# Moving GpSimd's two long additions, the softmax sums and half of the output projection inside one attention step

## The chip, the cores and the metric

The kernel runs on one core of one Trainium2 chip. The metric is device time in microseconds from the first to the last instruction and what lies around them. Each engine (TensorE, VectorE, ScalarE, GpSimd, SyncE for DMA issues) has its own instruction stream, written out by hand, and semaphores tie the streams together.

## The reference

64 independent blocks b, each of 256 rows by 256 columns, pass through cross attention over 120 context rows of 192 columns, and then through a quantised feed-forward layer (FFN):

```python
x = x + xattn(layernorm(x), ctx)       # 8 heads of 32: softmax(q k^T / sqrt(32)) v, then @ Wo + bo
x = x + ffn(layernorm(x))              # ln * g1 + b1n, int8-like rows, ternary w1 (1024), gelu,
                                       # ln * g2 + b2n, quantised rows, ternary w2, + b2
```

Quantising a row means dividing it by its largest absolute value over 127 and rounding.

## The kernel before

The program has two long stages. The attention stage takes steps i = -5 to 63, and every step works on several blocks at once, each at another point of its way. The FFN stage follows and is not touched by the change; between them stands a written-out piece for the last blocks. Steps 24 to 58 or so are in a hardware loop that holds four steps; the others are written out. In steps 4 to 21 some set-up work for the FFN weights is hung behind the steps ("aside").

One step of the attention stage, i, by engine, in the order of the code:

- TensorE (`attn` at the end of the file): raw scores of block i (L1237, `raw_ps` is signalled at their end), values of i-1 (L1264), projection of i-2 with Wo into `y_p` (L1317, `y_ps`), turning the partial maxima of i (L1244), softmax sums of i-1 (L1273, `sum_ps`), the shift that subtracts the maxima from the scores in PSUM (L1250, waits for `nmt_done`, signals `sc_ps`), keys and values of i+2 (`keys_values`: V's first product L1283, then K's from L1286, which wait for `x1_done`), queries of i+2 (L1307, `kvq_ps`), and the spreading of the inverse sums of i-1 (L1298).
- VectorE: the affine part of the FFN's layer norm of i-3 in two halves (L697, `h`), the maxima of the raw scores (L686, `nm_part`, waits for `raw_ps`), `h_max`, `nm_row`, `nm_t` (L724, which multiplies the maxima by the constant `block_sel`), the addition of `y_p` to the residual rows `xr` of i-2 (L730, waits for `y_ps`, signals `x1_done`), the inverse of the sums (L739), statistics, centring of `h` (L762), then `q_t` of i+2 (L774, waits for `kvq_ps`) and `o_t` of i-1 (L783).
- GpSimd: the inverse deviations of x of block i+3 (three small instructions L506, L508, L511, `r_done`), two additions over 512 columns, b2 to `xr` of i-3 (L489) and bo to `xr` of i-1 (L484), the quantisation of `h` of i-3 (L495, L497, waits for `h_scaled`), the power for `f_r` of i-2 (L525).
- ScalarE: copies, squares of x, the exponentials (L983, wait for `sc_ps`), `inv_hi`, the rounded rows.
- SyncE issues the DMAs in the order of its code: the turned rows, `ctx_t`, `xt`, `x_in`, then the store of `x_r` (waits for `r_done`), the load of `xr`, the store of `xr`, and the load of `r_bc`.

The PSUM bank of `y_p` is shared with `k_p`: K's products of i+2 may not start before VectorE has added `y_p` of i-2.

Of the kernel before, what the change touches and what calls it, by code (L numbers as in the profile page):

```python
# [49 lines left out]
def xattn_ffn(nc, KV, x, x_t, ctx_t_in, wq, wk, wv, wo, bo, ln1_g, ln1_b, w1, b1, ln2_g, ln2_b, w2, b2, out):  # L50
# [15 lines left out]
    with ExitStack() as ctx:  # L66
        def sb(name, shape, dt=F32, scope=ctx):
            return scope.enter_context(nc.sbuf_tensor(name, shape, dt))
# [20 lines left out]
        block_sel = sb("block_sel", [P, RB])  # L89
# [245 lines left out]
        with nc.Block() as block:  # L335
# [96 lines left out]
            def _(pool):  # L432
# [68 lines left out]
                def attn(i, n):  # L501
                    p, q = n % 2, 1 - n % 2
                    b = i + 3
# [8 lines left out]
                    b = i - 3  # L512
                    if live(b, NB):
                        add_b2(b, (n + 1) % 4)
                    b = i - 1
                    if live(b, NB):
                        add_bo(b, (n + 3) % 4)
# [84 lines left out]
            def _(dve):  # L602
# [16 lines left out]
                dve.tensor_reduce(block_sel[:, :], head_map[:, :, :, :].rearrange("p c j b -> p b c j"), AX.XY, ALU.add).then_inc(s_head, 1)  # L619
                dve.wait_ge(s_head, 3)  # L620
                dve.tensor_copy(head_sel[:, :, :], head_row[:, :].unsqueeze(2).to_broadcast([P, C, KP])).then_inc(s_head, 1)

# [507 lines left out]
            def _(pe):  # L1130
# [148 lines left out]
                def keys_values(b, p):  # L1279
# [3 lines left out]
                    pe.matmul(v_p, ctx_t[:, p, 0, 0:KV], w_kv[:, 1, :], start=True, stop=False)  # L1283
                    after(pe, x1_done, b - 3)
# [25 lines left out]

                def project(b, p):
                    pe.wait_ge(q_done, left(b + 4))
                    pe.wait_ge(k_done, left(b + 4))
                    pe.wait_ge(on_done, b + 1)
                    for t in range(T):
                        for c in range(C):
                            last = pe.matmul(y_p[:, t, :], o_t[:, p, c, t * P:(t + 1) * P],  # L1317
                                             wo_sb[:, c, :], start=(c == 0), stop=(c == C - 1))
                    last.then_inc(y_ps, 1)

                def attn(i, n):
# [5 lines left out]
                    if live(i - 1, NB):  # L1327
                        values(i - 1, (n + 3) % 4)
                    if live(i - 2, NB):
                        project(i - 2, p)  # L1330
                    if live(i, NB):
                        turn_minima(i)
                    if live(i - 1, NB):
                        sums(i - 1, q)
                    if live(i, NB):
                        shift(i)
                    if live(i + 2, NB):
                        keys_values(i + 2, p)
                        queries(i + 2, p)
# [79 lines left out]
```

## Time and profile before

| | us |
|---|---|
| median of 3 runs (lowest, highest) | 1227.91 (1223.06, 1230.76) |
| the profiled execution | 1227.72 |
| its span | 1226.0 |
| busy: VectorE, TensorE, ScalarE, GpSimd | 1128.3, 999.6, 815.4, 715.9 |

The granted clock of TensorE is 0.968 of full speed over the span. The attention stage is the part up to about 720 us, the FFN stage the rest. In the timelines below each line is the start in us from the span's start, the duration, the engine, the line of the code, the operation, the output and the inputs, the shapes, the count of merged instructions, and in brackets the idle time before it with what ended it.

### The profile page before, as it was taken

How to read it: one execution, taken by the hardware profiler on the slowest of the kernel's cores; microseconds unless marked ns; L12 is line 12 of the kernel's file. 1: busy time of each engine (PE TensorE's matmuls, PEld its weight loads, DVE VectorE, ACT ScalarE, POOL GpSimd, SP SyncE). 2: the span in 40 equal slices, each digit the busy share in tenths (PEclk: the TensorE clock that was granted, in tenths of full speed). 3: DMA queues.
4: the chain of work that ended last, by engine and by line, in shares of the span. 5: the costliest groups of instructions: out<-in, count | busy, mean ns of one | idle time of the engine just before them, and what ended most of it. 6: DMA issues, size and time to landing. Idle time of an engine off the chain costs nothing.

```text
span 1226.0 us, 29427 instructions
## 1 busy us (share of the span) xinstructions
PE 999.6 (82%) x9649; PEld 667.1 (54%) x9649; DVE 1128.3 (92%) x1718; ACT 815.4 (67%) x2083; POOL 715.9 (58%) x924
## 2 busy tenths in 40 slices
PE   5888888888888988888898876788777777777776
PEld 4566656656666666666666643444444444444444
DVE  2789998989999999999998989999999999999997
ACT  3555544555555555555554447799999999999993
POOL 3355644554555555555554544677777677767775
PEclk8999999989999999999999978899999999999998
DMA  5567765556666655666665430133222332233224
GB/s 141 137 149 149 164 133 107 133 111 132 141 141 135 130 127 134 137 136 140 135 136 115 100 91 18 26 36 42 35 34 34 40 37 34 34 39 38 34 35 69
DMA packets 144472, 114.63 MB, mean 93 GB/s; under 512 B 51580, under 2 KB 134908, under 8 KB 144408
## 3 DMA queue, kind: packets, MB, share of 16 engines
q1 hardware_dynamic: 126824, 96.90, 35.7%
q0 software_dynamic: 16864, 16.26, 11.2%
q8 instruction: 36, 0.59, 0.3%
q10 hardware_dynamic: 720, 0.66, 0.2%
q14 instruction: 28, 0.23, 0.1%
HBM read 71.75 MB, written 33.63 MB: 86 GB/s over the span
## 4 chain that ended last, share of the span: by engine, by line
DVE 43%; PE 30%; issue 24%; DVEq 1%; ACT 1%; POOL 1%; DMA 1%; POOLq 0%; ACTq 0%
DVE nm_part L686 11%; PE banks L1307 10%; DVE h L697 7%; DVE gn_low L810 6%; DVE gn_high L810 6%; PE banks L1273 5%; PE banks L1283 3%; DVE o_t L783 3%; PE banks L1286 2%; PE banks L1250 2%; DVE gn_low L796 2%; DVE gn_high L796 2%; PE banks L1288 2%; DVE q_t L774 1%; DVE g_max L816 1%
## 5 line engine op out<-in xcount | busy, mean ns | idle before, releaser
L983 ACT ACTIVATE probs<-banks 120x512 f32<-120x512 f32 x256 | 137.6, 590 | 168.7 <-PE banks L1250 168.7
L686 DVE TRANSPOSE_TENSOR_REDUCE nm_part<-banks 128x64 f16<-128x2048 f32 x64 | 147.4, 2302 | 3.5 <-PE banks L1237 3.2
L1021 ACT ACTIVATE g_dev<-g,g_sum 128x1024 bf16<-128x1024 f32 x128 | 149.1, 1165 | 0.0
L1026 ACT ACTIVATE g<-banks,h_dq 128x1024 f32<-128x1024 f32 x128 | 142.4, 1129 | 8.8 <-PE banks L1184 8.8
L1202 PE MATMUL banks<-w_t,g_t 128*128 128x256 bf16 x1008 | 125.2, 279 | 14.6 <-ACT g_t L1059 12.1
L495 POOL COPY h_dq<-h_cl 128x2 f32<-128x2 f32 (+1 forms) x64 | 13.7, 214 | 207.0 <-DVE h_qs L734 204.0
L1178 PE MATMUL banks<-w_t,h_t 128*128 128x512 bf16 x512 | 127.8, 394 | 2.0 <-ACT g L1026 1.3
L1307 PE MATMUL banks<-xt,wq_c 128*128 128x256 f32 x512 | 128.5, 394 | 0.0
L1317 PE MATMUL banks<-wo_sb,o_t 128*128 128x256 f32 x512 | 127.6, 392 | 1.0 <-DVE o_t L844 1.0
L1202 PEld LDWEIGHTS banks<-w_t,g_t 128*128 128x128 f16 x1008 | 95.7, 100 | 54.4 <-issue 26.9
L525 POOL TENSOR_TENSOR f_r<-f_ve,neg_half 128x2 f32<-128x2 f32 x62 | 50.0, 806 | 108.7 <-DVE f_ve L766 108.7
L1317 PEld LDWEIGHTS banks<-wo_sb,o_t 128*128 128x128 f32 x512 | 92.0, 189 | 37.3 <-issue 27.4
L558 POOL TENSOR_TENSOR g_r<-g_ve,neg_half 128x2 f32<-128x2 f32 x64 | 104.5, 1633 | 10.2 <-ACT g_ve L1042 10.2
L697 DVE SCALAR_TENSOR_TENSOR h<-h,f_r,b1n_bc 128x256 f32<-128x256 f32 x122 | 107.8, 923 | 0.1
L1307 PEld LDWEIGHTS banks<-xt,wq_c 128*128 128x128 f32 x512 | 92.7, 191 | 18.3 <-issue 0.9
L989 ACT ACTIVATE k_t<-banks 128x256 f32<-128x256 f32 x64 | 24.5, 383 | 114.1 <-DVE q_t L774 114.1
L484 POOL TENSOR_TENSOR xr<-xr,bo_bc 128x512 f32<-128x512 f32 x64 | 89.5, 1399 | 5.6 <-DMA xr<-in_x 5.6
L489 POOL TENSOR_TENSOR xr<-xr,b_bc 128x512 f32<-128x512 f32 x64 | 91.9, 1436 | 0.0
L533 POOL TENSOR_TENSOR g_dq<-g_max,w_out 128x2 f32<-128x2 f32 x64 | 12.5, 196 | 130.7 <-DVE gn_low L810 70.3
L774 DVE TENSOR_TENSOR q_t<-banks,r_bc 128x512 f32<-128x512 f32 x64 | 44.3, 692 | 47.7 <-PE banks L1307 38.8
L1244 PE MATMUL banks<-ident_h,nm_part 128*128 128x128 f16 x64 | 13.9, 217 | 88.0 <-DVE nm_part L686 88.0
L1196 PE MATMUL banks<-ident_h,gn_low 128*128 128x128 f16 x512 | 40.3, 224 | 51.2 <-POOL gn_low L538 51.2
(165 smaller groups left out, 2798.0 us busy)
## 6 DMA issues: line engine op xcount, KB each, us to landing
x_in<-in_x SPq DMA_DIRECT2D x64, 256.0 KB, 3.2
xt<-in_x_t SPq DMA_DIRECT2D x64, 256.0 KB, 2.9
xr<-in_x SPq DMA_DIRECT2D x64, 256.0 KB, 6.0
out<-xr SPq DMA_DIRECT2D x64, 256.0 KB, 6.2
out<-res POOLq DMA_DIRECT2D x62, 256.0 KB, 4.3
ctx_t<-in_ctx_t SPq DMA_DIRECT2D x64, 128.0 KB, 2.2
r_bc<-r_rows SPq DMA_DIRECT2D x64, 128.0 KB, 4.7
w_raw<-in_w_t SPq DMA_DIRECT2D x8, 256.0 KB, 5.4
```

The costliest lines, as they stand in the source:

```text
L489: pool.tensor_tensor(xr[:, r, :, :], xr[:, r, :, :], b2_bc[:, :].unsqueeze(1).to_broadcast([P, T, D]), ALU.add).then_inc(b2_done, 1)
L558: pool.tensor_tensor(g_r[:, q, :], g_ve[:, q, :], neg_half[:, 0:T], ALU.pow).then_inc(gr_done, 1)
L686: dve.tensor_reduce(nm_part[:, :, 0:C * RB], blocks_p, AX.X, ALU.max, negate=True, apply_transpose=True).then_inc(max_done, 1)
L697: last = dve.scalar_tensor_tensor(out=h[:, r1, t, :], in0=h[:, r1, t, :], scalar=f_r[:, q, t:t + 1], in1=b1n_bc[:, :], op0=ALU.mult, op1=A ...
L810: dve.scalar_tensor_tensor(out=gn[n][:, t, :], in0=gn[n][:, t, :], scalar=g_r[:, p, t:t + 1], in1=b2n_bc[:, :], op0=ALU.mult, op1=ALU.add) ...
L983: act.activation(probs[:, p, j, :, :], sc_p[0:KV, j, :, :], ACT.Exp, scale=SCALE).then_inc(probs_done, 1)
L1021: act.activation(g_dev[:, t, :], g[:, p, t, :], ACT.Square, scale=-float(F), bias=g_sum[:, p, t:t + 1], accum_out=g_ssq[:, p, t:t + 1]).th ...
L1026: act.activation(g[:, p, t, :], u_p[t], ACT.Gelu, scale=h_dq[:, b, t:t + 1], accum_out=g_sum[:, p, t:t + 1]).then_inc(gelu_done, 1)
L1178: pe.matmul(u_p[t][:, cols], h_t[:, b, t * C + c, :], w1_t[:, c, cols], start=(c == 0), stop=False, skip_group_check=True)
L1202: pe.matmul(y[t], turned_rows[:, t, f, :], w2_t[:, f, :], start=(first and f == 0), stop=False, skip_group_check=True)
L1307: last = pe.matmul(q_p[:, m, :], wq_c[:, c, m * P:(m + 1) * P], xt[:, p, c, :], start=(c == 0), stop=(c == C - 1))
L1317: last = pe.matmul(y_p[:, t, :], o_t[:, p, c, t * P:(t + 1) * P], wo_sb[:, c, :], start=(c == 0), stop=(c == C - 1))
```

## The change

Five edits:

1. GpSimd's additions of b2 and bo move to the head of its step, ahead of the three small instructions of x, and wait for `raw_ps` of this step.
2. TensorE's softmax sums of i-1 move up, directly behind the values of i-1.
3. The projection of i-2 is split by tile of 128 rows: tile 0 ahead of the turned maxima, tile 1 behind them. `y_ps` is signalled at the end of tile 1.
4. V's first product of i+2 moves ahead of the shift.
5. `block_sel` becomes 16-bit: `block_row` holds the 32-bit sums, and one more copy is made at the start.

```diff
@@ block_sel
-        block_sel = sb("block_sel", [P, RB])
+        block_row = sb("block_row", [P, RB])
+        block_sel = sb("block_sel", [P, RB], F16)
@@ gpsimd
                 def attn(i, n):
                     p, q = n % 2, 1 - n % 2
+                    if live(i, NB) and live(i - 1, NB):
+                        pool.wait_ge(raw_ps, i + 1)
+                    b = i - 3
+                    if live(b, NB):
+                        add_b2(b, (n + 1) % 4)
+                    b = i - 1
+                    if live(b, NB):
+                        add_bo(b, (n + 3) % 4)
                     b = i + 3
                     if live(b, NB):
                         pool.wait_ge(x_ssq, b * T + T)
...
                         pool.tensor_tensor(x_r[:, q, :], x_ve[:, q, :], neg_half[:, 0:T], ALU.pow).then_inc(r_done, 1)
-                    b = i - 3
-                    if live(b, NB):
-                        add_b2(b, (n + 1) % 4)
-                    b = i - 1
-                    if live(b, NB):
-                        add_bo(b, (n + 3) % 4)
@@ vector, at the start
-                dve.tensor_reduce(block_sel[:, :], head_map[:, :, :, :].rearrange("p c j b -> p b c j"), AX.XY, ALU.add).then_inc(s_head, 1)
+                dve.tensor_reduce(block_row[:, :], head_map[:, :, :, :].rearrange("p c j b -> p b c j"), AX.XY, ALU.add).then_inc(s_head, 1)
...
+                dve.tensor_copy(block_sel[:, :], block_row[:, :]).then_inc(s_head, 1)
+                dve.wait_ge(s_head, 5)
@@ tensor
-                def keys_values(b, p):
+                def first_values(b, p):
                     after(pe, q_done, b)
                     after(pe, v_done, b)
                     pe.wait_ge(ctx_loaded[p], (b - p) * 8 + 16)
                     pe.matmul(v_p, ctx_t[:, p, 0, 0:KV], w_kv[:, 1, :], start=True, stop=False)
+
+                def keys(b, p):
                     after(pe, x1_done, b - 3)
...
+                def project_tile(b, t, p):
+                    if t == 0:
+                        pe.wait_ge(q_done, left(b + 4))
+                        pe.wait_ge(k_done, left(b + 4))
+                        pe.wait_ge(on_done, b + 1)
+                    for c in range(C):
+                        last = pe.matmul(y_p[:, t, :], o_t[:, p, c, t * P:(t + 1) * P],
+                                         wo_sb[:, c, :], start=(c == 0), stop=(c == C - 1))
+                    if t == T - 1:
+                        last.then_inc(y_ps, 1)
...
                         values(i - 1, (n + 3) % 4)
+                        sums(i - 1, q)
                     if live(i - 2, NB):
-                        project(i - 2, p)
+                        project_tile(i - 2, 0, p)
                     if live(i, NB):
                         turn_minima(i)
-                    if live(i - 1, NB):
-                        sums(i - 1, q)
+                    if live(i - 2, NB):
+                        project_tile(i - 2, 1, p)
+                    if live(i + 2, NB):
+                        first_values(i + 2, p)
                     if live(i, NB):
                         shift(i)
                     if live(i + 2, NB):
-                        keys_values(i + 2, p)
+                        keys(i + 2, p)
                         queries(i + 2, p)
```

TensorE in one step of the loop, from the values to K's first products, before (in brackets the semaphores that an instruction waits for):

```order
L1264 MATMUL banks<-probs,v_sb 32x256 x7
L1317 MATMUL banks<-wo_sb,o_t 128x256 [waits on_done,k_done,q_done]
L1317 MATMUL banks<-wo_sb,o_t 128x256 x3
L1244 MATMUL banks<-ident_h,nm_part 128x128 [waits max_done,o_done]
L1273 MATMUL banks<-probs,sum_sel 32x128 [waits on_done]
L1273 MATMUL banks<-probs,sum_sel 32x128 x15
L1250 MATMUL banks<-nm_t,head_sel 128x256 [waits nmt_done]
L1250 MATMUL banks<-nm_t,head_sel 128x256 x7
L1283 MATMUL banks<-w_kv,ctx_t 120x256 [waits ctx_loaded0,v_done,q_done]
L1286 MATMUL banks<-ctx_t,w_kv 128x128 [waits x1_done]
```

The same stretch of the changed program, whose line numbers are a few higher:

```order
L1269 MATMUL banks<-probs,v_sb 32x256 x7
L1278 MATMUL banks<-probs,sum_sel 32x128 [waits on_done]
L1278 MATMUL banks<-probs,sum_sel 32x128 x15
L1324 MATMUL banks<-wo_sb,o_t 128x256 [waits on_done,k_done,q_done]
L1324 MATMUL banks<-wo_sb,o_t 128x256
L1249 MATMUL banks<-ident_h,nm_part 128x128 [waits max_done,o_done]
L1324 MATMUL banks<-wo_sb,o_t 128x256 x2
L1288 MATMUL banks<-w_kv,ctx_t 120x256 [waits ctx_loaded0,v_done,q_done]
L1255 MATMUL banks<-nm_t,head_sel 128x256 [waits nmt_done]
L1255 MATMUL banks<-nm_t,head_sel 128x256 x7
L1293 MATMUL banks<-ctx_t,w_kv 128x128 [waits x1_done]
```

Between the turned maxima and K's products there stood the 16 sum products, the shift and V's product; now two projection products, V's product and the shift stand there.

GpSimd in one step of the loop, before:

```order
L506 TENSOR_TENSOR x_var<-x_dev,inv_d 128x2 [waits x_ssq]
L508 TENSOR_TENSOR x_ve<-x_var,eps_t 128x2 [waits r_chain]
L511 TENSOR_TENSOR x_r<-x_ve,neg_half 128x2 [waits r_stored1,r_chain]
L489 TENSOR_TENSOR xr<-xr,b_bc 128x512 [waits h_centred]
L484 TENSOR_TENSOR xr<-xr,bo_bc 128x512 [waits xr_loaded1]
```

And in the changed program:

```order
L490 TENSOR_TENSOR xr<-xr,b_bc 128x512 [waits h_centred,raw_ps]
L485 TENSOR_TENSOR xr<-xr,bo_bc 128x512 [waits xr_loaded1]
L515 TENSOR_TENSOR x_var<-x_dev,inv_d 128x2 [waits x_ssq]
L517 TENSOR_TENSOR x_ve<-x_var,eps_t 128x2 [waits r_chain]
L520 TENSOR_TENSOR x_r<-x_ve,neg_half 128x2 [waits r_stored1,r_chain]
```

The two long additions are ahead of the three small instructions, and the first of them has the new wait.

## Rows read from the trace of the kernel before

**Rows 1.** The chain of waits, 363 to 378 us: start, us, what.

```profile
365.72 1.01 PE banks L1273 x32
...
368.81 1.94 PE banks L1307 x8
...
372.37 1.49 DVE h L697
```

**Rows 2.** Timeline of VectorE over one step of the loop, 363 to 378 us.

```profile
363.06 2.30 DVE L686 TRANSPOSE_TENSOR_REDUCE nm_part<-banks 128x64 f16<-128x2048 f32 x1
...
366.23 0.42 DVE L724 TENSOR_TENSOR nm_t<-nm_row,block_sel 128x256 f16<-128x256 f16 x1
366.57 0.68 DVE L730 TENSOR_TENSOR xr<-banks,xr 128x512 f32<-128x512 f32 x1
...
370.77 0.69 DVE L774 TENSOR_TENSOR q_t<-banks,r_bc 128x512 f32<-128x512 f32 x1 [0.29 <-PE banks L1307]
...
373.79 2.30 DVE L686 TRANSPOSE_TENSOR_REDUCE nm_part<-banks 128x64 f16<-128x2048 f32 x1
```

**Rows 3.** Timeline of TensorE's matmuls, same stretch.

```profile
365.65 1.08 PE L1273 MATMUL banks<-probs,sum_sel 120*32 120x128 f32 x32
366.71 0.40 PE L1250 MATMUL banks<-nm_t,head_sel 32*128 32x256 f16 x8
367.04 0.69 PE L1283 MATMUL banks<-w_kv,ctx_t 128*120 128x256 f32 x2
367.57 0.61 PE L1286 MATMUL banks<-ctx_t,w_kv 128*128 128x128 f32 x4
...
368.74 1.99 PE L1307 MATMUL banks<-xt,wq_c 128*128 128x256 f32 x8
370.57 0.39 PE L1298 MATMUL banks<-inv_part,spread 128*128 128x128 f16 x4
370.89 1.15 PE L1237 MATMUL banks<-q_t,k_t 32*128 32x256 f32 x16
...
376.24 0.22 PE L1244 MATMUL banks<-ident_h,nm_part 128*128 128x128 f16 x1 [1.28 <-DVE nm_part L686]
```

**Rows 4.** Timeline of VectorE, 371.95 to 372.2 and 372.5 to 373 us: the two halves of L697.

```profile
371.98 0.47 DVE L697 SCALAR_TENSOR_TENSOR h<-h,f_r,b1n_bc 128x256 f32<-128x256 f32 x1
...
372.37 1.49 DVE L697 SCALAR_TENSOR_TENSOR h<-h,f_r,b1n_bc 128x256 f32<-128x256 f32 x1
```

**Rows 5.** Timeline of GpSimd, same step.

```profile
367.49 0.18 POOL L495 COPY h_dq<-h_cl 128x2 f32 x1 [3.23 <-DVE h_qs L734]
...
371.63 0.69 POOL L511 TENSOR_TENSOR x_r<-x_ve,neg_half 128x2 f32<-128x2 f32 x1 [0.16 <-POOL x_ve L508]
372.29 1.30 POOL L489 TENSOR_TENSOR xr<-xr,b_bc 128x512 f32<-128x512 f32 x1
373.55 1.44 POOL L484 TENSOR_TENSOR xr<-xr,bo_bc 128x512 f32<-128x512 f32 x1
```

**Rows 6.** DMA issues: operation, count, size, us to landing.

```profile
xr<-in_x SPq DMA_DIRECT2D x64, 256.0 KB, 6.0
...
r_rows<-x_r SPq DMA_DIRECT2D x64, 1.0 KB, 4.6
```

**Rows 7.** Timelines of VectorE and GpSimd in an early step, 51.9 to 57 us.

```profile
51.92 0.69 DVE L774 TENSOR_TENSOR q_t<-banks,r_bc 128x512 f32<-128x512 f32 x1 [0.55 <-PE banks L1307]
...
53.13 2.94 DVE L697 SCALAR_TENSOR_TENSOR h<-h,f_r,b1n_bc 128x256 f32<-128x256 f32 x2
56.00 2.30 DVE L686 TRANSPOSE_TENSOR_REDUCE nm_part<-banks 128x64 f16<-128x2048 f32 x1
...
53.10 1.27 POOL L489 TENSOR_TENSOR xr<-xr,b_bc 128x512 f32<-128x512 f32 x1
```

**Rows 8.** Timelines of VectorE and GpSimd, 161 to 167 and 188 to 192.6 us.

```profile
162.11 0.69 DVE L774 TENSOR_TENSOR q_t<-banks,r_bc 128x512 f32<-128x512 f32 x1 [0.39 <-PE banks L1307]
...
166.34 2.30 DVE L686 TRANSPOSE_TENSOR_REDUCE nm_part<-banks 128x64 f16<-128x2048 f32 x1
...
188.54 0.69 DVE L774 TENSOR_TENSOR q_t<-banks,r_bc 128x512 f32<-128x512 f32 x1 [1.87 <-PE banks L1307]
...
191.66 2.31 DVE L686 TRANSPOSE_TENSOR_REDUCE nm_part<-banks 128x64 f16<-128x2048 f32 x1
...
188.39 1.27 POOL L489 TENSOR_TENSOR xr<-xr,b_bc 128x512 f32<-128x512 f32 x1
```

More of the change, by code:

```diff
@@ L1309, in queries @@
                     last.then_inc(kvq_ps, 1)
+                def project_tile(b, t, p):
[8 more added lines that the diff above has]
+                        last.then_inc(y_ps, 1)
                 def project(b, p):
-                    pe.wait_ge(q_done, left(b + 4))
-                    pe.wait_ge(k_done, left(b + 4))
-                    pe.wait_ge(on_done, b + 1)
                     for t in range(T):
[L1316 to L1319, printed above, removed]
+                        project_tile(b, t, p)
                 def attn(i, n):
```

## The prediction

> **What bounds the kernel now.** The busy shares name VectorE, but a share is an average, so I read the chain of waits first, in the middle of the hardware loop [rows 1]. There the chain changes hands twice a step: TensorE holds it from the turned maxima through the sums and the shift to the queries, VectorE from `q_t` over the second half of `h` (L697) to the maxima. The timelines of the same step give the lengths. One step is 373.79 - 363.06 = 10.73 us [rows 2]. Call T the end of the maxima, 363.06 + 2.30 = 365.36, and Q the start of `q_t`, 370.77. The half-step T to Q lasts 5.41 us and TensorE sets it: VectorE stands idle for 0.29 us ahead of `q_t` and the queries end that wait [rows 2]. The half-step Q to the next maxima lasts 3.02 us and VectorE sets it, and the maxima themselves take 2.30; TensorE waits 1.28 us there [rows 3]. So TensorE work that lies in the second half is free up to 1.28 us, TensorE work in the first half is not, and VectorE's first half has 0.29 us to spare.
>
> The two halves of `h` must be read one by one [rows 4]: the first takes 0.47 us, the second 1.49. GpSimd's addition of b2 runs from 372.29 to 373.59 [rows 5]; the second half starts at 372.37 and ends at 373.86, so it did nothing until the addition was over. That is 1.49 - 0.47 = 1.02 us of every step lost to a collision. The first half, started before the addition, lost nothing.
>
> **Edit 1, the additions.** Do they leave the collision? The new wait is for the scores, which run from 370.89 to 372.04 [rows 3], that is to Q + 1.27. An engine follows a signal 0.06 us later (end of `nm_t` at 366.65, shift at 366.71) to 0.15 us later (maxima at 365.36, first sum at 365.65 with the turned maxima between); I take 0.1, so the addition of b2 starts at about Q + 1.4. It starts now at Q + 1.52 [rows 2, 5]. The halves of `h` start at Q + 1.21 and Q + 1.60 [rows 4]. The wait thus puts the addition 0.1 us earlier, still behind the first half's start and ahead of the second's: the 1.02 us stays. The addition of bo stays under the maxima. Gain: nothing.
>
> What stands behind the new wait: the three small instructions of x now follow 2.7 us of additions. `r_done` moves from Q + 1.55 to about Q + 5.5. SyncE's queue has the store of `x_r`, then the load and the store of `xr`, then `r_bc` behind that signal, so all move by some 4 us. The load of `xr` needs 6.0 us to land [rows 6]: issued at about Q + 6.2, there at Q + 12.2, wanted by the addition of bo at Q + 10.7 + 2.7 = Q + 13.4. `r_bc` is issued once the store of `x_r` has landed, 4.6 us later, and its reader `q_t` is one and a half steps away. GpSimd itself idles 3.23 us ahead of the quantisation [rows 5], which covers the 1.3 us of small instructions. All of it is hidden; cost nothing. If the cover of `xr` (1.2 us) goes, the additions slip under `h_max` and cost nothing either until GpSimd's idle time is used up.
>
> **Edits 2 and 3, sums and projection.** The sums (1.01 us of the chain, [rows 1]) leave the first half, and tile 1 of the projection comes in. The queries are eight products of the same shape: 370.57 - 368.74 = 1.83 us, some 0.22 each and 0.1 more for the first, whose weights are loaded in the open [rows 3]. Tile 1 is four such products: 0.97 us. On TensorE alone this is a draw. In the second half the sums replace tile 1, also a draw, under the 1.28 us.
>
> But `y_ps` now comes at the end of tile 1. Tile 1 starts where the sums did, T + 0.29. Eight products need 370.77 - 368.74 = 2.03 us from their first start to VectorE's start behind them; four need 2.03 - 4 x 0.22 = 1.15. VectorE's addition L730 can start at T + 1.44 instead of T + 1.21 (366.57 - 365.36): late by 0.23. It takes 0.68, so `x1_done` comes at T + 2.12, and K's first product follows 0.06 later, at T + 2.18. It starts at T + 2.21 today [rows 3]. Its weights are then loaded in the open, 0.1 us as above. K, the other products and the queries keep their 3.20 us (370.77 - 367.57). So Q comes at about T + 2.28 + 3.20 = T + 5.5 instead of 5.41: **0.1 us longer a step.** TensorE's own road would be shorter (edit 4), but it waits for VectorE. VectorE, late by 0.23, uses up 0.23 of its idle 0.29 and stays ahead of the queries, which are late too.
>
> **Edit 4, V's product.** It takes 0.53 us (367.57 - 367.04) and moves from behind the shift to before it [rows 3]. The sums' last products and the shift leave a hole of about 0.1 us now, since the shift follows `nm_t`; with tile 1 and V ahead, the shift starts at T + 0.29 + 0.97 + 0.43 = T + 1.7, well behind `nm_t` at T + 1.29. TensorE would be at K by T + 2.0, which is 0.2 us earlier than today, and waits there for `x1_done`. The gain lands on that wait. The exponentials start 0.35 us later; ScalarE has over 1 us idle a step, so nothing.
>
> **Edit 5, 16 bits.** `nm_t` takes 0.42 us for 256 columns with one 32-bit input [rows 2]. Shorter or not, VectorE then waits at L730 for `y_ps`, so it counts zero. 
>
> **The early steps.** In six steps before 280 us TensorE was slow or late, and the addition of b2 began before the scores were done and was over before `h`. One is the step at 188: b2 from 188.39 to 189.66, and 191.66 - 188.54 = 3.12 us from `q_t` to the maxima. A step with the same work in which b2 met `h` took 166.34 - 162.11 = 4.23 [rows 8]. The new wait makes the first kind into the second: at most 1.1 us each, at least nothing. I take 0.7 x 6 = 4 us (bounds 0 and 6.6).
>
> **Sum.** Of 64 steps some 57 have all the parts: 57 x 0.1 = 6 us. With 4 us in the early steps: +10 us on the profiled 1227.72, which is the median of the runs (1227.91) within 0.2. Forecast 1237 us. The step's term has bounds of -0.05 (weights loaded under the wait: Q at T + 5.38) and +0.2 (VectorE starts later behind `y_ps`), so -3 to +11 us, and with the early steps 1225 to 1246.
>
> **Rival A: the collision goes** (faster). Should the addition of b2 begin behind the second half of `h`, VectorE has 1.02 us less a step, and TensorE's slack of 1.28 covers it: 57 x 1.02 = 58 us, 1170. For it: the maxima and the addition now wait for the same signal. Against it: the signal comes 0.33 us ahead of the second half. Chance 0.07.
>
> **Rival B: both halves collide** (slower). If `q_t` falls 0.15 us or more behind the scores, the addition starts ahead of the first half, bo takes the second, and nothing is left under the maxima. The step at 52 us shows it [rows 7]: b2 at 53.10, `h` at 53.13, both halves 2.94 us, 56.00 - 51.92 = 4.08 us from `q_t` to the maxima instead of 3.02. Price 1.06 x 57 = 60 us, 1298; in the ten or so written-out full steps alone, 1248. It decides at 0.1 to 0.2 us of lateness of VectorE against the queries; I have it 0.1 ahead. The Trainium skill, "SBUF — State Buffer", section on who interferes with whom, says that a VectorE instruction with two SBUF inputs and a reading GpSimd instruction exclude each other for a whole instruction, and that issue order decides; rows 4 and 7 agree with it (0.47 and 1.49 us in one order, 2.94 in the other). Chance 0.11 for all of it or the written-out part.
>
> **Rival C: the wait for `y_ps` is shorter than I have it** (faster). Should L730 not be late, the 0.2 us of edit 4 come through: 57 x 0.19 = 11 us less, with the early steps 1221. It needs tile 1 to take 0.25 us less than the queries' products of the same shape. Chance 0.17.
>
> **Clock.** The mean granted clock is 0.968; a stretch at the lower level (1.2 instead of 2.4 GHz) costs a few us, and a change in TensorE's gaps can add or drop one. That is 5 us either way inside each case.
>
> **How the numbers follow.** Forecast (1225 to 1246) 0.55, C 0.17, B 0.11, A 0.07, things I did not see 0.10. A range from 1214 to 1258 holds the forecast, C, the small form of B and half of the unseen, 0.8. This kernel's measurement tells about 1% from no change, 12 us: 1215.6 to 1240.2. Forecast 0.36 within and 0.19 above; C 0.11 within, 0.06 below; A 0.07 below; B 0.10 above; the unseen in thirds. Faster 0.20, same 0.48, slower 0.32.
>
> **What would show it.** In the profile after: a step of 10.8 us in the loop; the second half of `h` still at 1.5 us with b2 starting at Q + 1.4; L730 with some 0.2 us idle ahead of it that tile 1 ends; K's first product behind L730; six early steps longer. A second half of `h` at 0.47 us proves A, a first half over 1 us proves B, a step under 10.6 with no wait at L730 proves C.

## The result and the profile after

| | before | changed |
|---|---|---|
| median, us (lowest, highest, runs) | 1225.5 (1223.06, 1230.76, 4) | 1241.26 (1239.48, 1247.94, 4) |
| ratio [95% interval] | | 1.0133 [1.0084, 1.0183] |
| the profiled execution, its span | 1227.72, 1226.0 | 1247.94, 1246.3 |
| granted clock over the span | 0.968 | 0.960 |

The kernel is 1.3% slower, 16 us by the medians. The profiled execution of the changed kernel is its slowest, and its granted clock, 0.960, is the lowest measured for this kernel (0.963 to 0.968 in its other executions). So the 20.3 us between the two spans are 4.5 more than the medians give, and what is said below of the clock's share holds for this execution. I read the two traces against each other, stage by stage first.

A step is named here by the block whose `q_t` begins it. The stretches run from one `q_t` to another: blocks 5 to 24 (written out), 24 to 58 (the loop, and two steps ahead of it) and 58 to 63. Columns are length, busy us of TensorE's matmuls, its weight loads, VectorE, ScalarE and GpSimd, then the granted clock, the DMA share and GB/s. Before:

```profile
65.35:284.48 219.13, 187.70 (x2001) 134.24 (x1999) 199.34 (x395) 115.10 (x327) 114.65 (x170) 0.96 0.64 136
284.48:649.94 365.46, 321.45 (x3572) 229.61 (x3570) 346.19 (x681) 200.35 (x579) 192.16 (x307) 1.00 0.62 134
649.94:706.21 56.27, 48.72 (x527) 34.66 (x525) 51.62 (x104) 25.82 (x69) 30.28 (x53) 0.97 0.49 107
```

The same stretches of the changed kernel:

```profile
61.19:294.03 232.84, 193.47 (x2001) 136.17 (x1999) 207.75 (x396) 114.10 (x327) 121.45 (x174) 0.93 0.59 129
294.03:663.22 369.19, 321.21 (x3572) 229.05 (x3570) 350.71 (x681) 198.05 (x579) 197.25 (x306) 1.00 0.59 133
663.22:724.75 61.53, 52.94 (x527) 37.23 (x525) 52.85 (x105) 25.55 (x69) 31.39 (x53) 0.89 0.50 101
```

The loss is not in the loop, where most of the steps are (+3.7 us over 34 steps), but in the written-out steps on both sides of it (+13.7 and +5.3), and there the granted clock is lower. Ahead of block 5 the changed kernel gains 4.2 us: 2.6 of them in the step at 52 us, where both halves of `h` had collided [rows 7] and which now has b2 behind the first half, and 1.6 before it. Behind block 63 another 1.8 us are added, which is no more than the kernels below differ by there (517.4 to 521.5 us).

**The loop step.** The chain of waits, start, us and what, answering [rows 1], changes hands at the same places:

```profile
381.05 1.94 PE banks L1314 x8
...
384.61 1.50 DVE h L702
```

VectorE in one step of the loop, answering [rows 2]; then TensorE, answering [rows 3]:

```profile
375.26 2.30 DVE L691 TRANSPOSE_TENSOR_REDUCE nm_part<-banks 128x64 f16<-128x2048 f32 x1
...
378.43 0.42 DVE L729 TENSOR_TENSOR nm_t<-nm_row,block_sel 128x256 f16<-128x256 f16 x1
...
378.95 0.69 DVE L735 TENSOR_TENSOR xr<-banks,xr 128x512 f32<-128x512 f32 x1
...
383.01 0.69 DVE L779 TENSOR_TENSOR q_t<-banks,r_bc 128x512 f32<-128x512 f32 x1
...
386.04 2.30 DVE L691 TRANSPOSE_TENSOR_REDUCE nm_part<-banks 128x64 f16<-128x2048 f32 x1
```

```profile
377.71 0.22 PE L1249 MATMUL banks<-ident_h,nm_part 128*128 128x128 f16 x1 [1.28 <-DVE nm_part L691]
377.76 1.08 PE L1324 MATMUL banks<-wo_sb,o_t 128*128 128x256 f32 x4
...
379.21 0.40 PE L1255 MATMUL banks<-nm_t,head_sel 32*128 32x256 f16 x8
...
379.70 0.71 PE L1293 MATMUL banks<-ctx_t,w_kv 128*128 128x128 f32 x4
```

T is 375.26 + 2.30 = 377.56 and Q is 383.01. The addition L735 (L730 before) starts at T + 1.39 instead of T + 1.21; it ends at 379.64 and K's first product follows at 379.70. The step is 10.78 us long (10.77 on average), 0.04 over the one before. TensorE's wait ahead of the turned maxima is 1.28 us, as before.

The halves of `h`, answering [rows 4], and GpSimd, answering [rows 5]:

```profile
384.22 0.47 DVE L702 SCALAR_TENSOR_TENSOR h<-h,f_r,b1n_bc 128x256 f32<-128x256 f32 x1
...
384.61 1.50 DVE L702 SCALAR_TENSOR_TENSOR h<-h,f_r,b1n_bc 128x256 f32<-128x256 f32 x1
```

```profile
384.38 1.45 POOL L490 TENSOR_TENSOR xr<-xr,b_bc 128x512 f32<-128x512 f32 x1 [0.96 <-PE banks L1242]
...
387.84 0.71 POOL L520 TENSOR_TENSOR x_r<-x_ve,neg_half 128x2 f32<-128x2 f32 x1 [0.16 <-POOL x_ve L517]
```

The addition of b2 now waits for the scores and starts at Q + 1.37, and the second half of `h` still stands behind it for 1.50 us.

**An early step.** VectorE, GpSimd and TensorE between 171 and 184 us, to be held against [rows 8]:

```profile
171.68 0.69 DVE L779 TENSOR_TENSOR q_t<-banks,r_bc 128x512 f32<-128x512 f32 x1 [0.28 <-PE banks L1314]
...
175.85 2.30 DVE L691 TRANSPOSE_TENSOR_REDUCE nm_part<-banks 128x64 f16<-128x2048 f32 x1
...
180.49 0.69 DVE L735 TENSOR_TENSOR xr<-banks,xr 128x512 f32<-128x512 f32 x1 [1.04 <-PE banks L1324]
...
174.19 1.45 POOL L485 TENSOR_TENSOR xr<-xr,bo_bc 128x512 f32<-128x512 f32 x1
...
178.30 0.27 PE L1249 MATMUL banks<-ident_h,nm_part 128*128 128x128 f16 x1 [2.53 <-DVE nm_part L691]
178.37 2.02 PE L1324 MATMUL banks<-wo_sb,o_t 128*128 128x256 f32 x4
```

In these steps set-up work stands ahead of `h`, so it is addition bo, not b2, that takes the second half. The maxima start 4.17 us behind `q_t`, as in the step at 162 before (4.23). TensorE then waits 2.53 us, and behind that wait its products take twice their time (four of L1324: 2.02 us instead of 1.08): it has been granted 1.2 GHz instead of 2.4. So L735 waits 1.04 us more, and the step takes 13.4 us.

### The profile page after: what moved, and what is told of

Same layout as the page of the kernel before. It is cut to its first block, busy times and chain, and to the rows that moved or that the text cites. A ratio compares the mean times of both kernels' runs of the same rounds, so it can differ in the third digit from the quotient of the medians.

```text
span 1246.3 us, 29490 instructions
## 1 busy us (share of the span) xinstructions
PE 1007.4 (81%) x9649; PEld 671.1 (54%) x9649; DVE 1139.0 (91%) x1719; ACT 812.8 (65%) x2083; POOL 715.0 (57%) x924
## 4 chain that ended last, share of the span: by engine, by line
DVE 47%; PE 25%; issue 23%; POOL 3%; DVEq 1%; DMA 1%; ACT 0%; POOLq 0%; ACTq 0%
DVE nm_part L691 11%; PE banks L1314 10%; DVE h L702 8%; DVE gn_low L815 6%; DVE gn_high L815 6%; PE banks L1324 4%; PE banks L1293 4%; DVE o_t L788 3%; DVE xr L735 3%; DVE gn_high L801 2%; PE banks L1295 2%; POOL gn_high L541 1%; DVE gn_low L801 1%; DVE q_t L779 1%; PE banks L1297 1%
## 5 line engine op out<-in xcount | busy, mean ns | idle before, releaser
L1324 PE MATMUL banks<-wo_sb,o_t 128*128 128x256 f32 x512 | 149.6, 418 | 0.9 <-DVE o_t L849 0.9
L490 POOL TENSOR_TENSOR xr<-xr,b_bc 128x512 f32<-128x512 f32 x64 | 98.4, 1537 | 63.6 <-PE banks L1242 63.6
L702 DVE SCALAR_TENSOR_TENSOR h<-h,f_r,b1n_bc 128x256 f32<-128x256 f32 x122 | 115.8, 990 | 0.1
L1324 PEld LDWEIGHTS banks<-wo_sb,o_t 128*128 128x128 f32 x512 | 91.2, 198 | 22.0 <-issue 14.0
L561 POOL TENSOR_TENSOR g_r<-g_ve,neg_half 128x2 f32<-128x2 f32 x64 | 91.4, 1428 | 10.3 <-ACT g_ve L1047 10.3
L801 DVE SCALAR_TENSOR_TENSOR gn_low<-g,g_nm,g_bc 128x1024 f32<-128x1024 f32 x64 | 81.3, 1277 | 0.0
```

Source lines behind the costliest of these rows:

```text
L490: pool.tensor_tensor(xr[:, r, :, :], xr[:, r, :, :], b2_bc[:, :].unsqueeze(1).to_broadcast([P, T, D]), ALU.add).then_inc(b2_done, 1)
L702: last = dve.scalar_tensor_tensor(out=h[:, r1, t, :], in0=h[:, r1, t, :], scalar=f_r[:, q, t:t + 1], in1=b1n_bc[:, :], op0=ALU.mult, op1=A ...
L801: dve.scalar_tensor_tensor(out=gn[n][:, t, :], in0=g[:, p, t, :], scalar=g_nm[:, p, t:t + 1], in1=g2_bc[:, :], op0=ALU.add, op1=ALU.mult). ...
```

## Where the 20 us are

Two things can be summed over the steps of the two traces: the time from `q_t` to the maxima, which a collision lengthens, and the time at the lower clock. The price of the latter comes from experiment 5 below: 0.39 us for each us. A collision is one of the two long additions of GpSimd holding up a half of `h`.

| stretch | longer, us | `q_t` to maxima, sum | time at 1.2 GHz | worked out |
|---|---|---|---|---|
| blocks 5 to 14 | 0.5 | | none in either | 9 steps of 0.05 |
| 14 to 24 | 13.3 | 36.5 to 43.2 | 17.1 to 34.1 | 6.8 + 17.0 x 0.39 = 13.4 |
| 24 to 58 | 3.7 | +1.1 in one step | 0 to 3.4 | 1.1 + 1.3 + 33 x 0.04 = 3.7 |
| 58 to 63 | 5.3 | +1.5 in one step | 3.4 to 13.6 | 1.5 + 4.0 = 5.5 |

The two prices hold beyond the pair of kernels that gave them. From block 14 to 24 the length of the stretch runs from 107.9 to 135.6 us over the fourteen profiles of this document; less the sum from `q_t` to the maxima and less 0.39 us for each us at 1.2 GHz it is 78.7 to 79.9 us in every one.

The one loop step is that of block 29, whose `q_t` is at 348.00 us. The loop's first pass ends there:

```profile
349.41 3.02 DVE L702 SCALAR_TENSOR_TENSOR h<-h,f_r,b1n_bc 128x256 f32<-128x256 f32 x2
...
349.46 1.28 POOL L490 TENSOR_TENSOR xr<-xr,b_bc 128x512 f32<-128x512 f32 x1 [1.04 <-PE banks L1242]
...
354.81 0.22 PE L1249 MATMUL banks<-ident_h,nm_part 128*128 128x128 f16 x1 [2.61 <-DVE nm_part L691]
```

Both halves collide there, as in rival B, and the step takes 13.46 us. `q_t` is not late against the scores: they end at Q + 1.26, as in every loop step. It is `h` that comes late, at Q + 1.41 instead of 1.20, and it does so in the kernel before as well. So the addition, at Q + 1.45, began 0.044 us behind the first half's start by the records, and still went ahead of it.

## Experiments

All are compared with the kernel before on their own chip; its medians were 1225.54, 1224.21 and 1227.64 us in the three groups of runs. Times of stretches come from each kernel's profiled execution.

**1. Edit 1 alone.** The kernel before with GpSimd's new order and wait, nothing else:

```diff
+                    if live(i, NB) and live(i - 1, NB):
+                        pool.wait_ge(raw_ps, i + 1)
+                    b = i - 3
+                    if live(b, NB):
+                        add_b2(b, (n + 1) % 4)
...
```

> The kernel before with edit 1 alone (the two additions at the head of GpSimd's step, behind the scores). Theory: edit 1 costs nothing in the loop (step 10.73 us, second half of h 1.49 us as before) and carries most of the loss through the steps before 280 us, where the additions now meet h: 1234 to 1240 us, and the maxima start about 4.2 us behind q_t in the steps with weight work, not 3.1 to 3.6. Rival: the loss comes from TensorE's new order (edits 2 to 4), and this kernel takes 1224 to 1229 us.

Measured: 1238.03 us, as expected, ratio 1.0109 [1.0082, 1.0136]. Loop steps take 10.73 us, as before; blocks 5 to 24 take 231.4 us instead of 219.1, blocks 58 to 63 59.5 instead of 56.3. VectorE, then GpSimd, in a loop step:

```profile
379.08 0.69 DVE L776 TENSOR_TENSOR q_t<-banks,r_bc 128x512 f32<-128x512 f32 x1 [0.29 <-PE banks L1309]
...
382.10 2.30 DVE L688 TRANSPOSE_TENSOR_REDUCE nm_part<-banks 128x64 f16<-128x2048 f32 x1
...
380.45 1.44 POOL L489 TENSOR_TENSOR xr<-xr,b_bc 128x512 f32<-128x512 f32 x1 [1.12 <-PE banks L1239]
```

The addition starts at Q + 1.37 and the maxima at Q + 3.02: nothing is won in the loop, and the written-out steps lose.

This trace prices the clock without any added work. The step of block 17 has the same collision and the same wait of TensorE (2.53 us) as that of block 15, but no time at 1.2 GHz: it takes 11.98 us against 13.56 with 3.4 us at that level, 0.46 us lost for each us. So the lower level does not follow every such wait either.

**2. The other edits alone.** The changed kernel with edit 1 undone (the hunk of experiment 1 reversed, so that the three small instructions stand ahead of the additions again).

> The changed kernel with edit 1 undone (GpSimd as before; sums, projection, V's product and the 16-bit constant as changed). Theory: the loop's step is 10.77 us instead of 10.73 from the wait for tile 1 ahead of L730, which makes 2 to 3 us in all: 1227 to 1231 us, early steps as before. Rival: TensorE's order carries the loss, 1236 to 1242 us, with the lower clock as often as in the changed kernel.

Measured: 1210.51 us, 0.9881 [0.986, 0.9903]. My expectation failed: this half of the change is a gain of 1.2%, which edit 1 takes away. Blocks 5 to 24 are longer than before (226.2 us), but the loop takes 343.7 us instead of 365.5. Two steps of it, VectorE and then GpSimd:

```profile
508.65 0.69 DVE L777 TENSOR_TENSOR q_t<-banks,r_bc 128x512 f32<-128x512 f32 x1
...
509.86 0.87 DVE L700 SCALAR_TENSOR_TENSOR h<-h,f_r,b1n_bc 128x256 f32<-128x256 f32 x2
...
518.40 0.69 DVE L777 TENSOR_TENSOR q_t<-banks,r_bc 128x512 f32<-128x512 f32 x1
...
519.61 1.94 DVE L700 SCALAR_TENSOR_TENSOR h<-h,f_r,b1n_bc 128x256 f32<-128x256 f32 x2
...
510.32 1.55 POOL L490 TENSOR_TENSOR xr<-xr,b_bc 128x512 f32<-128x512 f32 x1
...
519.98 1.28 POOL L490 TENSOR_TENSOR xr<-xr,b_bc 128x512 f32<-128x512 f32 x1
```

In the first step b2 starts at Q + 1.67 and both halves together take 0.87 us; in the second at Q + 1.58 and they take 1.94. The second half of `h` starts at Q + 1.60. GpSimd's small instructions follow work of VectorE that comes behind L730, and L730 is 0.18 us later while Q is only 0.04 later: that moves the addition from Q + 1.52 to the edge of the collision. Some 23 of the 34 steps are clear of it and take 9.75 us, the others 10.83.

**3. The addition behind `h`, in the kernel before.** One line ahead of the addition of b2:

```diff
+                        pool.wait_ge(h_affine, b + 1)
                         add_b2(b, (n + 1) % 4)
```

> The kernel before, with the addition of b2 made to wait until both halves of h of the same block are done (h_affine), nothing else changed. Theory: the collision is worth its full 1.02 us a step, since TensorE has 1.28 us to spare there: step 9.7 us, both halves 0.47 us, about 58 us less, 1165 to 1175 us. Rival: something else takes over after a part of it (the additions run into the next work of GpSimd, or TensorE's queue), and a step is 10.2 us or more, 1195 us or more.

Measured: 1163.24 us, 0.9487 [0.9461, 0.9513], a little under the expected range. VectorE, GpSimd and TensorE in the loop:

```profile
466.96 0.69 DVE L775 TENSOR_TENSOR q_t<-banks,r_bc 128x512 f32<-128x512 f32 x1 [0.29 <-PE banks L1308]
...
468.17 0.87 DVE L698 SCALAR_TENSOR_TENSOR h<-h,f_r,b1n_bc 128x256 f32<-128x256 f32 x2
...
469.12 1.27 POOL L489 TENSOR_TENSOR xr<-xr,b_bc 128x512 f32<-128x512 f32 x1 [0.59 <-DVE h L698]
...
471.41 0.22 PE L1245 MATMUL banks<-ident_h,nm_part 128*128 128x128 f16 x1 [0.26 <-DVE nm_part L687]
...
476.68 0.69 DVE L775 TENSOR_TENSOR q_t<-banks,r_bc 128x512 f32<-128x512 f32 x1 [0.29 <-PE banks L1308]
```

The step is 476.68 - 466.96 = 9.72 us. The 1.02 us of the collision are gone, TensorE's wait falls from 1.28 to 0.26 by the same amount, and the addition of b2 runs under the maxima at no cost: it takes 1.27 us beside them. Rival A's price was right; its condition is not one that the change makes.

**4. The same in the changed kernel**, in place of the wait for the scores:

```diff
-                    if live(i, NB) and live(i - 1, NB):
-                        pool.wait_ge(raw_ps, i + 1)
                     b = i - 3
                     if live(b, NB):
+                        pool.wait_ge(h_affine, b + 1)
                         add_b2(b, (n + 1) % 4)
```

> The changed kernel with its wait for the scores replaced by the same wait for both halves of h. Theory: the additions' place at the head of the step is harmless and the signal was the wrong one: both halves 0.47 us, step 9.75 us, 1168 to 1180 us, some 4 us behind the kernel before with that wait. Rival: with the small instructions of x behind the additions, r_done and the load of xr come too late once the step is 9.7 us, and GpSimd waits for the load; then 1190 us or more.

Measured: 1163.22 us, 0.9496 [0.9475, 0.9518], the same as experiment 3 and 5 us below the expected range. Loop steps take 9.75 us instead of 9.72. So edits 2 to 5 show no gain of their own once the collision is gone; what they did in experiment 2 was to move the addition. Between the two kernels stands the semaphore for which b2 waits: 1241 us with the scores, 1163 with `h`.

**5. Work in TensorE's gap.** To tell the clock from the collisions, the changed kernel computes tile 0 of the projection three times instead of once in the written-out steps 12 to 22, 60 and 61. Nothing is left out; the two copies overwrite the same values, and TensorE has less time to wait.

```diff
                         project_tile(i - 2, 0, p)
+                        if isinstance(i, int) and (12 <= i <= 22 or i in (60, 61)):
+                            project_tile(i - 2, 0, p)
+                            project_tile(i - 2, 0, p)
```

> The changed kernel with tile 0 of the projection computed twice more in steps 12 to 22, 60 and 61: the same values into the same place, 1.9 us of TensorE work ahead of the turned maxima, where it waited over 2.5 us in those steps. Theory: the lower clock follows these waits; with work in them it stays high in the early steps, and each of some nine early steps is 2.5 us shorter, minus up to 0.5 us where the added work ends too late: 15 to 25 us less than the changed kernel, 1216 to 1227 us. Rival: the collisions of the additions alone make the loss and the clock falls as often for other reasons: 1241 us or more.

Measured: 1229.69 us, 1.0025 [1.0003, 1.0046]. That is 11.6 us less than the changed kernel by the medians, where I expected 15 to 25: the direction was right and the size too large. Blocks 5 to 24:

```profile
62.54:283.58 221.04, 199.20 (x2089) 145.68 (x2087) 207.85 (x396) 113.91 (x327) 120.92 (x174) 0.99 0.65 135
```

TensorE does 88 products more, as the trace counts them, and the stretch is 11.8 us shorter than in the changed kernel, with a granted clock of 0.99 instead of 0.93. The collisions are unchanged: from block 14 to 24 the sum from `q_t` to the maxima is 43.2 and 43.3 us, while the time at 1.2 GHz is 3.4 us instead of 34.1 and the stretch 123.7 us instead of 135.6. That is 11.9 / 30.7 = 0.39 us lost for each us at the lower level. TensorE in one of these steps:

```profile
178.48 0.22 PE L1249 MATMUL banks<-ident_h,nm_part 128*128 128x128 f16 x1 [0.80 <-DVE nm_part L691]
...
178.53 1.08 PE L1324 MATMUL banks<-wo_sb,o_t 128*128 128x256 f32 x4
```

The wait is 0.80 us instead of 2.53 and tile 1 takes 1.08 instead of 2.02.

**6. Edit 1 only from step 24 on**, in the changed kernel: `late = not isinstance(i, int) or i >= 24` decides whether the additions stand at the head with the wait or behind the small instructions.

> The changed kernel, with edit 1 in force from step 24 on only (before it GpSimd keeps the old order without the wait). Theory: in the loop edit 1 pins the addition of b2 to Q + 1.37, ahead of the second half of h, so every loop step stays at 10.77 us; the early steps lose less TensorE time and less clock than in the changed kernel, 5 to 10 us: 1231 to 1237 us. Rival: the loss against the kernel with TensorE's edits alone (1210) is made in the early steps, and this kernel takes 1210 to 1218 us.

Measured: 1235.78 us, 1.009 [1.0054, 1.0125]. Blocks 5 to 24 take 228.6 us, so only 4.2 of the 13.7 come back: the other edits lengthen these steps too, as experiment 2 showed (226.2; the code of these steps is the same, so 2.4 us is what two profiles of it differ by). In experiment 1 edit 1 alone made them 231.4. Each edit is enough to move the addition out of the lucky places that it had before in four of these steps (b2 over before `h` began), and the losses don't add. In the step of block 29 both halves collided again.

**7. Additions at the head, no wait**, in the kernel before: edit 1's hunk without its first two lines.

> The kernel before with the two additions at the head of GpSimd's step and no wait for the scores. Theory: the addition of b2 begins right behind f_r, at about Q + 0.3, and ends at Q + 1.6; the first half of h (Q + 1.2) waits for its end, the addition of bo then meets the second half: the two halves take 2.0 to 2.4 us together, a step 10.8 to 11.2 us, 1228 to 1250 us. Rival: the addition of b2 is over before it hurts and bo alone collides as b2 did: step 10.73, 1223 to 1228 us.

Measured: 1214.41 us, 0.9928 [0.99, 0.9956]. I expected slower. VectorE and GpSimd in the loop:

```profile
502.91 1.98 DVE L697 SCALAR_TENSOR_TENSOR h<-h,f_r,b1n_bc 128x256 f32<-128x256 f32 x2
...
501.94 1.26 POOL L489 TENSOR_TENSOR xr<-xr,b_bc 128x512 f32<-128x512 f32 x1
...
503.16 1.45 POOL L484 TENSOR_TENSOR xr<-xr,bo_bc 128x512 f32<-128x512 f32 x1
```

`q_t` starts at 501.71. b2 is nearly over when `h` begins, and bo takes the second half: one collision with another partner, and the loop step is 10.83 us (the stretch 24 to 58 is 3.3 us longer than before). The gain is in the written-out steps (213.2 us for blocks 5 to 24, 52.0 for 58 to 63), where the additions are often over before `h`. So over the whole it is edit 1's wait, not its order, that costs. In two steps it is the order: at blocks 19 and 20 the three small instructions had held b2 back behind `h` (Q + 3.6 and 4.0), and without them ahead of it the additions collide in this kernel too.

**8 to 10. How late must the addition be?** Small fillers ahead of b2 in the kernel before: a `memset` of two columns, one copy of two columns, two such copies.

```diff
+        pad = sb("pad", [P, 8, 2])
...
+                        pool.tensor_copy(pad[:, n, :], neg_half[:, 0:T])
                         add_b2(b, (n + 1) % 4)
```

> The kernel before with one more instruction on GpSimd ahead of the addition of b2 in every step: a memset of 2 columns into an unused tile. Theory: in the loop the addition of b2 starts at Q + 1.52 and wins against the second half of h at Q + 1.60; in the kernel with TensorE's edits alone it started at Q + 1.67 and lost. Some 0.1 to 0.2 us of added work brings it over that line: loop steps of 9.72 us where it starts after Q + 1.65, 20 to 40 us less in all (1186 to 1206 us), while the written-out steps still collide. Rival: the order on the port is not a matter of a tenth of a us, and the kernel takes 1224 to 1230 us.

> The same with one copy. Theory: b2 starts at Q + 1.65 to 1.7 in three of four loop steps and at Q + 1.58 in the fourth and at Q + 1.5 in the written-out ones, so 20 to 26 of the steps lose the collision and the others keep it: 1190 to 1210 us. Rival: no line there: either all steps clear (below 1180) or none (above 1220).

> The kernel before with two more GpSimd instructions ahead of the addition of b2 in every step (copies of 2 columns into an unused tile, 0.15 us or so each). The memset of the earlier run moved the addition by 0.05 us only and so tested nothing. Theory: b2 starts at Q + 1.65 (written-out steps) to Q + 1.8 (loop), behind the second half of h, and nearly all steps fall to 9.7 us: 1165 to 1185 us, by work added to an engine. Rival: an addition that starts close behind still holds the second half up: 1215 us or more.

Measured: `memset` 1229.03 us, 1.0027 [1.0003, 1.0051]; one copy 1185.28, 0.9647 [0.961, 0.9684]; two copies 1179.05, 0.9597 [0.9574, 0.962]. VectorE and GpSimd with the `memset`, then with one copy:

```profile
499.47 0.69 DVE L776 TENSOR_TENSOR q_t<-banks,r_bc 128x512 f32<-128x512 f32 x1 [0.29 <-PE banks L1309]
...
500.67 1.91 DVE L699 SCALAR_TENSOR_TENSOR h<-h,f_r,b1n_bc 128x256 f32<-128x256 f32 x2
...
501.03 1.28 POOL L490 TENSOR_TENSOR xr<-xr,b_bc 128x512 f32<-128x512 f32 x1
```

```profile
483.39 0.69 DVE L776 TENSOR_TENSOR q_t<-banks,r_bc 128x512 f32<-128x512 f32 x1 [0.29 <-PE banks L1309]
...
484.60 0.87 DVE L699 SCALAR_TENSOR_TENSOR h<-h,f_r,b1n_bc 128x256 f32<-128x256 f32 x2
...
485.08 1.52 POOL L490 TENSOR_TENSOR xr<-xr,b_bc 128x512 f32<-128x512 f32 x1
```

The `memset` moved the addition by 0.05 us only, to Q + 1.56, still ahead of the line, and so says nothing of where the line is. One copy moved it to Q + 1.69, and every loop step is clear and takes 9.72 us: now the addition waits for `h` (its record is 1.52 instead of 1.27 us long). I had expected 20 to 26 clear steps. With two copies it starts at Q + 2.08 and takes 1.27. That is not twice the delay: the second copy itself starts at Q + 1.67, behind the second half of `h`, and waits for it, so its record is 0.45 us long where the first one's is 0.22. Both kernels keep collisions in the early steps, where set-up work moves `h` and a fixed delay does not follow it; that is why neither reaches experiment 3.

**11. Edit 4 on top of experiment 3**: V's first product ahead of the shift, the sums where they were.

```diff
+                    if live(i + 2, NB):
+                        first_values(i + 2, p)
                     if live(i, NB):
                         shift(i)
                     if live(i + 2, NB):
-                        keys_values(i + 2, p)
+                        keys(i + 2, p)
```

> The kernel before with the wait for both halves of h (1163 us), plus edit 4 alone: V's first product ahead of the shift. y_ps stays early, so K's first product is not held back. Theory: the hole of 0.1 us between the sums and the shift closes and K starts at T + 2.05 to 2.12 instead of 2.21: a step of 9.56 to 9.65 us, 5 to 9 us less, 1154 to 1159 us. Rival: VectorE, which had 0.29 us to spare ahead of q_t, or the exponentials on the way to inv_hi take the gain: 1161 us or more.

Measured: 1171.65 us, 0.9569 [0.9539, 0.9598], 8 us slower than experiment 3 where I expected a gain. TensorE:

```profile
379.08 0.69 PE L1284 MATMUL banks<-w_kv,ctx_t 128*120 128x256 f32 x2
...
379.71 0.40 PE L1251 MATMUL banks<-nm_t,head_sel 32*128 32x256 f16 x8
...
380.03 0.71 PE L1289 MATMUL banks<-ctx_t,w_kv 128*128 128x128 f32 x4
...
381.31 1.99 PE L1310 MATMUL banks<-xt,wq_c 128*128 128x256 f32 x8
```

V's product is no free filler behind the sums. It starts at T + 1.30, the shift behind it at T + 1.93 instead of T + 1.35 and K at T + 2.26 instead of T + 2.21, and 1.28 instead of 1.17 us pass from K to the queries. The step is 0.15 us longer, 9.87.

**12. Experiment 4 without edit 4**: V's product back behind the shift.

> The changed kernel with the wait for both halves of h (1163 us, step 9.75 us) and edit 4 undone: V's first product behind the shift again. Theory: K's weights can be loaded behind V's product while x1_done is awaited, which gives back the 0.1 us that K's open load costs, and V fills the wait: a step of 9.70 to 9.72 us, 1160 to 1163 us. Rival: V's product ahead of the shift was a gain, and this step is 9.8 us or more, 1167 us or more.

Measured: 1172.62 us, 0.9536 [0.9511, 0.9562]. Most loop steps take 9.75 us, as in experiment 4, and not the 9.70 to 9.72 that I expected. V's place is worth nothing in the loop, as the prediction had it: K's first product starts at T + 2.21 with V between the shift and K, and at T + 2.13 with V ahead of the shift (experiment 4), but K's second starts at T + 2.35 in both.

The time is all the same some 10 us above the expected range and 9 us above experiment 4. Part of that is seen in the trace. GpSimd waited for the load of `xr` eight times between 100 and 570 us, for up to 1.22 us, where experiment 4 has one such wait of 0.23, and four steps of the loop stretch are 0.04 to 0.64 us longer than their neighbours. The late load, hidden in a step of 10.7 us, has next to no slack left in one of 9.75. Whether edit 4 or the other group of runs brings these waits is open.

## Why it came out so, step by step

The forecast was 1237 and the median 1241.26; the time lay inside the range, but 1% or more slower was not the likeliest of the three outcomes. That the number came so near is partly luck. The loop's term was 4 us too large, the gain of 4.2 us ahead of block 5 was not forecast, and the starting point, 1227.91 from three executions, was 2.4 us above the median of four; together they hid much of a clock term that was missing. The change itself was forecast at 10 us and is 15.8 by the medians, 20.3 in the profiles. By the steps of the prediction:

- **Edit 1 in the loop: right.** b2 at Q + 1.37 (forecast 1.4), the second half at 1.50 us, nothing gained. Experiment 1 isolates it.
- **What is queued behind the wait: right in the loop.** `x_r` ends at 387.84 + 0.71, Q + 5.5. GpSimd sat idle ahead of the addition of bo for the load of `xr` twice in the whole trace, both times in the first 44 us (17.0 us against 5.6 before); block 5 is reached 4.2 us earlier all the same.
- **Edits 2 to 4: right in the steps, too large in the sum.** L735 at T + 1.39 (forecast 1.44), K at T + 2.14 (2.18), the shift at T + 1.65 (1.7), Q at T + 5.45 (5.5). Each was some 0.05 us early, so the step grew by 0.04 and not 0.1: 2 us, not 6. Tile 1 began at T + 0.20, not at T + 0.29. (The lower bound of this term, Q at T + 5.38, is 0.03 us under 5.41 and not 0.05.)
- **Edit 5: right.** `nm_t` takes 0.42 us with both inputs of 16 bits, as before. The Trainium skill, "VectorE: DVE Perf Modes", section "What auto-detection actually checks", asks for 16 bits and a step of one in every tensor; the 0.42 us agree with it, since `block_sel` is read with a step of zero.
- **The early steps: right for the six steps counted, too small for the stretch.** The term was "0.7 x 6 = 4 us (bounds 0 and 6.6)". In the six steps of the kernel before that fit its description (blocks 5, 15, 16, 18, 22, 23) the time from `q_t` to the maxima grew by 4.0 us in all. But blocks 19 and 20, which had been clear because b2 came behind `h`, got one and two collisions, 3.3 us; they were not in the count. From block 14 to 24 the collisions make 6.8 us of the 13.3, and one step in the loop and one behind it (block 60) came on top, 1.1 and 1.5 us.
- **The clock: mis-stated, and the largest term missing.** I put it as 5 us either way, independent of the cases. It was tied to the early steps' term and had one sign: a collision in a step that is already long leaves TensorE waiting 2.5 us, and mostly TensorE runs at 1.2 GHz behind that wait. From block 14 to 24 this makes 6.6 of the 13.3 us, and from block 5 to 63 some 12 us (30.7 us more at the lower level, by the table). Experiment 5 takes 11.8 us away with these collisions left in place. That is what carried the result over 1%.
- **Rival B: its picture once, not its condition.** In the step of block 29 both halves collided because `h` was 0.2 us late behind `q_t`, not because `q_t` was late against the scores. Its price per step (1.06 us) was 1.1 by `q_t` to the maxima, and with the clock the step is 2.7 us over its neighbours.
- **Rival A: its condition missed, its price right.** 1170 forecast, 1163 measured in experiments 3 and 4. From block 5 to 24 experiment 3 has 6.8 us at the lower clock instead of 17.1, which at 0.39 is 4 of the 7 us more.

What the prediction did not see at all is that edits 2 to 5 alone are faster (experiment 2): I compared the addition with `h` for edit 1 only, and not for the edits that shift VectorE and with it GpSimd. And its chances do not add up as they stand: its own shares give 0.16 for faster and 0.51 for the same, where it says 0.20 and 0.48.

Open: in these profiles 64 stretches at 1.2 GHz begin between 60 and 640 us, and 52 of them inside a TensorE wait of 2 us or more or within 2 us behind it. The others, such as those at 181.5 and 225.9 us of experiment 3, have only shorter waits near them (1.68 and 1.75 us there). And the same wait did not always bring one, as experiment 1 showed.

## What to carry to other kernels

Where an instruction of one engine is far over its usual time, find what it collides with, and put the two in order by a semaphore of the victim, not by one that happens to come at about the same time: here the scores come at Q + 1.3 and `h` at Q + 2.1, and that is the difference between +1% and -5%. Before costing a shift of some tenths of a microsecond, mark every pair of colliding instructions and ask on which side of the edge the shift leaves each. And price a longer wait of TensorE together with the clock that follows it, not as a separate uncertainty.

## What the runs showed of the hardware

- **The edge of the collision is sharp, and just behind the recorded start of VectorE's instruction.** With the second half of `h` starting at Q + 1.60 by its record, an addition that started at Q + 1.62 or before went first and cost it 1.0 to 1.1 us; at Q + 1.66 or later it came second and cost nothing (0.48 us for the half, and the addition's own record grew from 1.27 to 1.5 us). Taken over both halves and all fourteen profiles, 211 times an addition started between 0.10 us before and 0.15 us behind a half. Up to 0.050 us behind, it always went first; from 0.053 us on it came second, but for one case at 0.060. The Trainium skill, "SBUF — State Buffer", section "Who interferes with whom", says that a VectorE instruction with two SBUF inputs contends with a GpSimd instruction that reads SBUF, and that issue order decides who blocks; the runs agree. No run here shows why the line lies where it does.
- **Exclusion depends on the partner.** The addition beside the maxima, which read PSUM, took 1.27 us and the maxima 2.31 (experiment 3). Maxima with no addition beside them took 2.30, and the one addition of that kernel with nothing of VectorE beside it took 1.26.
- **The clock fell behind long waits.** Of 42 waits of TensorE of 2.5 us or more between 60 and 640 us in these profiles, 37 had a stretch at 1.2 GHz begin in them or within 2 us behind, and each us of it cost 0.39 us (experiment 5) to 0.46 (two steps of experiment 1).
- **Two more columns of work can be free or not.** A `memset` of two columns moved GpSimd's next instruction by 0.05 us, a copy of the same size by 0.17; a second copy took 0.45 us because it met `h`.
